# The last layer's output product in three F32R terms, with a new order at the end of each tile

## The reference

```python
qkv = x @ W_qkv                      # x: layer norm of the first layer's result
bq = bq * cos + rotate_half(bq) * sin     # the same for bk, keys of this window and the one before
sim = einsum('bhwid,bhwjd->bhwij', bq, bk)      # masked
attn = softmax(sim)
s = einsum('bhwij,bhwjd->bhwid', attn, bv) ... @ W_out      # [.., 1024] @ [1024, 256]
g = silu(sum over the two chosen experts of w * (x @ We[expert]))
x = x + s * g
```

## Time and profile before

| | us |
|---|---|
| median of three runs | 2545.28 (2543.22 to 2546.12) |
| the profiled execution | 2545.65 |
| its span | 2544.0 |
| PE busy in the span | 2329.7 (92%) |
| DVE busy | 1814.1 (71%) |
| ACT busy | 1488.3 (59%) |
| POOL busy | 968.4 (38%) |
| the last layer, from its first load to the end of the span | 1451.35 to 2544.0 |

### The profile page before, as it was taken

The page is one execution under the profiler, slowest core; times in us unless marked ns, Lnnn a source line. Parts: engine busy times, 40 slices in busy tenths (PEclk is TensorE's granted clock), DMA queues, the critical chain, the costliest instruction groups (busy, mean ns, idle before and its releaser), DMA issues. The chain is left out here.

```text
span 2544.0 us, 42440 instructions
## 1 busy us (share of the span) xinstructions
PE 2329.7 (92%) x14884; PEld 1481.5 (58%) x14884; DVE 1814.1 (71%) x4382; ACT 1488.3 (59%) x2938; POOL 968.4 (38%) x971
## 2 busy tenths in 40 slices
PE   5879999999999999969977589999999999999998
PEld 4722333333333333248866477777778777777777
DVE  7888888887878787424427677777777777777775
ACT  3525556665656566756534266666666666666665
POOL 3431111111111212124426255555666555555564
PEclk9869999999999999989987699999999999999999
DMA  4770223150505050033327300000000000000000
GB/s 131 228 151 14 29 40 45 27 63 22 65 20 65 20 65 21 7 127 119 137 95 248 116 11 15 15 15 10 13 15 15 15 15 15 15 15 15 12 14 10
DMA packets 139953, 133.08 MB, mean 52 GB/s; under 512 B 48740, under 2 KB 128106, under 8 KB 139747
## 3 DMA queue, kind: packets, MB, share of 16 engines
q1 hardware_dynamic: 107395, 98.01, 16.8%
q10 hardware_dynamic: 26848, 15.73, 2.4%
q0 software_dynamic: 5504, 16.69, 1.8%
HBM read 83.90 MB, written 46.14 MB: 51 GB/s over the span
## 5 line engine op out<-in xcount | busy, mean ns | idle before, releaser
L929 DVE TENSOR_REDUCE a_best<-a_ring 128x1 f32<-128x512 f32 (+3 forms) x1280 | 699.7, 603 | 153.6 <-PE a_ring L736 99.8
L841 ACT ACTIVATE a_probs<-a_pss 128x1024 f32<-128x1024 f32 (+3 forms) x640 | 556.3, 896 | 394.6 <-PE a_pss L783 380.8
L695 POOL TENSOR_SCALAR_AFFINE_SELECT a_probs<-a_probs 128x256 f32<-128x256 f32 x256 | 102.9, 408 | 791.1 <-ACT a_probs L841 789.3
L1808 ACT ACTIVATE w_probs<-w_pss,w_top 128x256 f32<-128x256 f32 x512 | 238.5, 471 | 264.5 <-DVE w_top L1893 164.5
L1644 POOL TENSOR_TENSOR w_probs<-w_probs,w_inv 128x512 f32<-128x512 f32 x256 | 311.5, 1217 | 164.5 <-DVE w_inv L1901 157.2
L1675 PE MATMUL w_psw<-wqkv,w_xr 128*128 128x512 f32 x1152 | 299.8, 397 | 10.3 <-POOL w_xr L1604 10.3
L1893 DVE CUSTOM_DVE_ANT_0 w_pss<-w_pss,w_masks 128x256 f32<-128x256 f32 x512 | 208.6, 449 | 127.0 <-PE w_pss L1706 127.0
L736 PE MATMUL a_ring<-g_kb,g_qa 96*128 96x512 bf16 (+3 forms) x640 | 229.4, 373 | 28.6 <-DVE a_best L929 16.8
L736 PE MATMUL a_ring<-a_kb,a_qa 96*128 96x512 bf16 (+3 forms) x640 | 220.2, 353 | 19.1 <-DVE a_best L929 14.8
L1675 PEld LDWEIGHTS w_psw<-wqkv,w_xr 128*128 128x128 f32 x1152 | 206.3, 191 | 44.9 <-POOL w_xr L1604 10.8
L783 PE MATMUL a_pss<-g_qa,g_kb 99*128 99x512 bf16 (+3 forms) x640 | 219.0, 355 | 2.3 <-DMA g_qa<-a_neg_rows 2.1
(11 more groups left out here) (226 smaller groups left out, 4269.3 us busy)
## 6 DMA issues: line engine op xcount, KB each, us to landing
e_w<-in_w SPq DMA_DIRECT2D x16, 1024.0 KB, 7.9
qk_parts<-p_parts SPq DMA_DIRECT2D x32, 384.0 KB, 3.4
g_qa<-qk_parts SPq DMA_DIRECT2D x96, 64.0 KB, 13.3
a_kb<-qk_parts SPq DMA_DIRECT2D x24, 256.0 KB, 9.1
a_qa<-qk_parts SPq DMA_DIRECT2D x96, 64.0 KB, 13.6
g_kb<-qk_parts SPq DMA_DIRECT2D x18, 256.0 KB, 8.7
v_rows<-p_vout SPq DMA_DIRECT2D x8, 512.0 KB, 4.5
expert_in<-zero POOLq DMA_DIRECT2D x16, 256.0 KB, 4.0
```

What stands on the lines that cost most here:

```text
L841: act.activation(probs[:, idx % 4, :, lo:CH], pss[idx % 2][:, :, lo:CH], ACT.Exp).then_inc(exp_done, 1)
L929: vec.tensor_reduce(best[:, i // TC, h * TC + i % TC, k:k + 1], bank[:, 0:keys], X, ALU.max).then_inc(ring_taken, 1)
L1808: ins = act.activation(probs[:, p % 4, e, :], pss[p % 2][:, e, :], ACT.Exp, bias=top[:, e, p:p + 1], scale=-1.0, accum_out=rows[:, e, p:p ...
```

## The change

It has these parts:

- `wout` becomes two F32R tensors. SP loads w_out as pieces 10 and 11, ACT rounds them at the turn of the last chunk, behind pieces 8 and 9, and POOL subtracts. The one transfer of 1 MB goes.
- `ot` becomes two F32R tensors. The copy out of `pso` is a step of its own, O0 and O1: ACT rounds, DVE subtracts, and only DVE's part lets PE go on. OUT is 24 F32R products in place of 8 F32 ones.
- The rotation writes into `raw`; `rot` goes. ACT's copies of W wait for the turns R that read `raw`, the rotation no longer waits for them.
- `res` goes: the gating writes into `sig`, POOL adds into `x1`, and SP stores from there; ACT's load of x1 waits for the store of two tiles before.
- The end of a tile becomes O0 N7 R0 T5 E2 PV4 T6 R1 PV5 T7 R2 PV6 X PV7 O1 E3 R3 G OUT. The order up to PV3 stays.

```diff
-        piece_turns = {0: (0, 1, 2), 1: (3, 4, 5), NC - 2: (6, 7), NC - 1: (8, 9)}
+        for n in range(2):
+            some = slice(n * PAIRS // 2, (n + 1) * PAIRS // 2)
+            pieces.append((io["w_out"][n * H * DH // 2:(n + 1) * H * DH // 2, :].rearrange("(k p) d -> p k d", p=P),
+                           *(keep["wout"][r][:, some, :].rearrange("p k d -> p (k d)") for r in range(2))))
+        piece_turns = {0: (0, 1, 2), 1: (3, 4, 5), NC - 2: (6, 7), NC - 1: (8, 9, 10, 11)}
...
-            sp.dma_start(keep["wout"][:, :, :], io["w_out"].rearrange("(k p) n -> p k n", p=P)).then_inc(wout_landed, 16)
...
+STEP_ORDER = ("S0 W0 S1 N0 W1 S2 N1 W2 S3 N2 W3 QR0 T0 S4 N3 W4 QR1 QR2 KR0 T1 PV0 S5 N4 W5 QR3 QR4 KR1 KR2 T2 PV1 "
+               "S6 N5 E0 QR5 KR3 T3 PV2 S7 N6 E1 KR4 KR5 T4 PV3 O0 N7 R0 T5 E2 PV4 T6 R1 PV5 T7 R2 PV6 X PV7 O1 E3 "
+               "R3 G OUT")
...
-                return eng.tensor_tensor(rot[:, r, half].rearrange("p (h x) -> p h x", x=DH // 2),
+                return eng.tensor_tensor(src[:, half].rearrange("p (h x) -> p h x", x=DH // 2),
...
-            return eng.tensor_tensor(rot[:, r, half], rot[:, r, half], crossed[:, r, half], ALU.add)
+            return eng.tensor_tensor(src[:, half], src[:, half], crossed[:, r, half], ALU.add)
...
-                        pool.tensor_tensor(res[:, u, :], res[:, u, :], x1[:, u, :], ALU.add).then_inc(out_ready, 1)
+                        pool.tensor_tensor(x1[:, u, :], sig[:, :], x1[:, u, :], ALU.add).then_inc(out_ready, 1)
...
-                            ins = pe.matmul(psw[bank][:, 0:D], ot[:, p, :], wout[:, p, :], start=(p == 0), stop=(p == PAIRS - 1))
+                            for a, b in PARTS:
+                                ins = pe.matmul(psw[bank][:, 0:D], ot[a][:, p, :], wout[b][:, p, :],
+                                                start=(p == 0 and (a, b) == PARTS[0]),
+                                                stop=(p == PAIRS - 1 and (a, b) == PARTS[-1]))
...
-                    wait(act, (q_rotated, k_rotated)[n // 2], 2 * (t + 1))
+                    if t >= 0:
+                        act.wait_ge(t_ready, turns.filled(t - 1, ("R", 2 * (n % 2) + n // 2), ("T", "R")))
...
-                wait(act, out_ready, t - 1)
+                wait(act, stored[u], 16 * i)
...
-                    elif s[0] == "PV" and s[1] % 4 == 3:
-                        half = s[1] // 4
-                        wait(act, pv_done, PAIRS * t + s[1] + 1)
+                    elif s[0] == "O":
+                        half = s[1]
+                        wait(act, pv_done, PAIRS * t + 4 * half + 4)
...
-                        act.copy(ot[:, 4 * half:4 * half + 4, :], pso[:, :, :]).then_inc(ot_ready, 1)
+                        act.copy(ot[0][:, 4 * half:4 * half + 4, :], pso[:, :, :]).then_inc(ot_high, 1)
...
-                    wait(vec, t_ready, BEFORE_TURNS + TURNS * t)
...
+                    elif s[0] == "O":
+                        half = s[1]
+                        four = slice(4 * half, 4 * half + 4)
+                        vec.wait_ge(ot_high, 2 * t + half + 1)
+                        vec.tensor_tensor(ot[1][:, four, :], pso[:, :, :], ot[0][:, four, :].bitcast(F32), ALU.subtract
+                                          ).then_inc(ot_ready, 1)
...
-                        vec.scalar_tensor_tensor(out=res[:, u, :], in0=psw[work.bank(t, s)][:, 0:D], scalar=0.5, in1=sig[:, :],
+                        vec.scalar_tensor_tensor(out=sig[:, :], in0=psw[work.bank(t, s)][:, 0:D], scalar=0.5, in1=sig[:, :],
```

## The result

| | before | after |
|---|---|---|
| median us (lowest to highest, runs) | 2544.25 (2541.82 to 2546.12, 4) | 2526.70 (2525.19 to 2533.28, 4) |
| profiled execution, its span | 2545.65, 2544.0 | 2533.28, 2531.5 |
| join, first load to the last layer's first load | 132.07 | 136.06 |
| last layer, to the end of the span | 1092.65 | 1073.51 |
| of it, up to the last OUT but one | 1059.28 | 1036.95 |

The ratio is 0.9937 (0.9917 to 0.9956). The profiled execution is the slowest of the four after. Its join begins 2.65 us later than before, behind stages that the change doesn't touch; that belongs to neither kernel.

What follows compares the result with a forecast made beforehand. PE, busy 98%, bounded each tile before; afterwards the chain over DVE would end last. 2545.3 - 9.5 (last layer) + 3.7 (join) = 2539.5 us, range 2529 to 2551.

Steps and rivals of the forecast that it cites:

- the two gaps: Last layer, each tile: new PE waits before W1 (released by gating) and before S2 (by ACT's exponential), about 0.5 us each.
- E3's start: Tile end on PE: distances between operations from PV3 on add up to 7.57 us when E3 starts.
- the last tile: Last layer's final tile: PE alone sets the end; 0.15 us from T7's copy and 0.6 in OUT, about 0.8 won.
- given back from S2 to the next PV3: Following tile: ACT is late with W0's copy, which holds W2 by 0.03 us.
- gain per tile: Each of 30 last-layer tile boundaries: S2 at 17.23 instead of 17.56 us after PV3, 0.33, taken as 0.30 us.
- The subtraction: DVE's new step after O1's copy: 0.69 us, low end 0.43, high end 1.42; priced at 0.72 in the chain.
- The slower rival: Each tile boundary: the subtraction takes 1.4 us, 0.65 per boundary beyond the gain, 2568 us in all; chance 0.08.
- The boundary ahead of it: Boundary to the last tile: R2's low halves on DVE hold O1, S0's maximum starts later, 0.3 us lost.
- The clock: Rival, every tile: more PE idling lowers the granted clock, some 1 us a tile, 2570 us; chance 0.02.
- The join: Ahead of the last layer: ACT's two extra casts +2.0 us, POOL holding the routing's second instruction +1.7, together +3.7.
- the side of no gain: Rival: tiles gain nothing, E3's start or a link being 0.3 us longer; only the join's cost remains, 2549 us; chance 0.20.
- PE's own gain: OUT on PE, each tile: 24 one-pass products instead of 16 records give back about 0.3 to 0.6 us.

Runs made afterwards that it cites:

- the change again: The full change run once more, unaltered, beside the kernel before on the same chip: 2530.02 us, ratio 0.9941.

## Why the prediction was wrong

The mechanism was right: the chain E3, X, O1, subtraction, y, R3's copies, low halves, G, gating, maximum, exponential, S2 sets the tile. The doubled subtraction shows it, and the two gaps stand where they were foretold. What failed are sizes in it, E3's start above all, and the last tile.

| step of the forecast | forecast | measured |
|---|---|---|
| E3's start after PV3 | 7.57 | 7.26 |
| E3 to X | 1.69 | 1.69 |
| X to O1, O1 to the subtraction | 0.43, 0.62 | 0.43, 0.62 |
| subtraction to y | 0.72 | 0.61 |
| y to R3's copies, to its low halves | 1.04, 0.87 | 1.02, 0.88 |
| low halves to S0's maximum, to the exponential | 2.27, 0.95 | 2.22, 0.94 |
| exponential to S2 | 1.07 | 1.08 |
| sum | 17.23 | 16.75 |
| given back from S2 to the next PV3 | 0.03 | 0.13 |
| gain per tile | 0.30 | 0.68 |

- **E3's start** is the step that failed most, "after a PV 0.59 ... R to PV 0.58. For T to R no row is free of a wait; I take 0.52". The sum counted PV6 and PV7 at 1.18 together. The pair takes 1.03 (0.15 less), each of two T to R 0.49 (0.06 in all), each of two R to PV 0.53 (0.10). The run with PV6 and PV7 apart puts the pitches back, and the period goes to 32.99. So 0.31 of the chain's 0.48 error stands here. The 0.58 for R to PV was read from the right pair of neighbours, but what stands ahead of the pair differs: in the earlier trace rows R2 comes behind a wait and R3 behind a PV, in the new order R comes behind T. In the kernel before each value product whose transposes follow a projection starts 0.52 to 0.54 behind them, and each whose transposes follow a value product 0.58 to 0.59.
- **The subtraction** of 0.69 overlaps with the y behind it: 0.61. Where a second subtraction follows it, the distance is 0.73, about what the sum had (0.72). Each row of it above takes 0.69. The slower rival's price was about right, though not its condition: 0.65 us more per boundary was put at 19 us, and the doubled subtraction brought 20.6 us for 0.71.
- **The gain per tile.** The 30 periods between the first tile's OUT and the last but one are 33.395 us long on average before and 32.689 after: 30 x 0.706 = 21.2 of the 22.3 us that the layer is shorter up to there. Forecast were 9.0. The other 1.1 us are OUT's earlier place in the first tile; they are given back at the other end, where OUT is earlier and S2 is not.
- **The last tile** "about 0.8 won" is the second wrong step. From its S2 to the end it is 2.0 us longer (29.15, before 27.11), since PE has half the clock for some 9 us of it. The boundary ahead of it, "0.3 lost", lost 0.03 (16.51 from PV3 to S2, before 16.48); with the 1.1 us of OUT's earlier place these make the 3.2 of the first table (36.56 and 33.37 after the last OUT but one). The clock was among the rivals as a cost of every tile; I had not asked it of the one tile where PE has no other work. That it fell is in part luck of the execution: it fell in the old last tile as well in another run (29.26), and the part behind S2 was 26.8 to 27.3 in four runs with the new order.
- **The join**: 3.6 of 3.7, both terms, parted by two runs.
- **Sum.** -22.3, +3.2 and +3.6 are -15.5; the medians differ by 17.5, the ratio's interval spans 11 to 21 us. The chunk loop of the join ahead of the routing differs by some us from one execution to the next also with equal code (join 136.06 and 131.71 us in two executions of the changed kernel), and the last tile by some 2 us, so the remaining 2 us are not told from that.
- **The range** was too narrow for its own sum. The text said that every 0.1 us of the chain is 3 us, but only the side of no gain got a case from it; distances that were estimated, or read where something else stood ahead, could be wrong the other way as well.
- Of PE's own gain, "0.3 to 0.6" for OUT was 0.34, and none of it is seen in the time: the kernel before with the new order alone is 17 us faster (20 beside the change again in its own group). There a tile takes 32.18, after the change 32.69: what the product wins on PE, its subtraction loses on a chain that ends last, and the join's 3.6 us come with it. The addition into x1 in place of `res` was not run by itself; it is no part of the chain above.

## What to carry to other kernels

Price an order and an arithmetic change apart: here the order alone was worth 36 us and the product that is cheaper on PE lost about half of them, since it loads DVE, through which the chain ends. Take the distance between two PE instructions only from a row with the same pair of neighbours and the same instruction ahead of them; a term that recurs 30 times needs both its ends in the range, on both sides. Look at the last tile by itself, since a wait that other work hides in every other tile stands open there, and read the granted clock in more than one execution before you put its fall down to a change.

## What the runs showed of the hardware

- Two value products (eight 64-column F32 matmuls each) side by side follow at 0.44 us (1.03 for the pair, less the 0.59 to the next operation), but with transposes between them at 0.58 to 0.59 on each side. Four transposes are followed by a value product after 0.53 when a projection or other transposes stand ahead of them, and after 0.58 when a value product does.
- The same idle time of PE brings the granted clock down in one place and not in another. Behind a gap of 2.54 us (the change with the old order) it fell to 0.50 in 22 of 30 tiles and stayed at 1.00 in 8; in the last tile, with 1.59 us ahead of S2, it stayed at 1.00 before (the next product takes 0.38, not 0.58) and fell some 2 us behind the start of S2 with the rotation in place. Behind 3.2 to 3.4 us in the last tile it fell in all eight profiled executions. It was then at the lower level for 3 to 10 us.
- A DVE and a POOL subtraction with two SBUF inputs at the same time: two of DVE take 4.91 us in place of 2.35, two of POOL 5.67 in place of 4.67. The Trainium skill ("SBUF — State Buffer", Who interferes with whom) states that such a pair exclude each other; the rows agree, and so do the 2.10 and 0.42 of the routing's second instruction.
